# Level 0 of a gated linear attention moved between the last value and gate tiles of the sequence before, with the orders of the other engines

## The reference

```python
q, k, v, gate projections of layernorm(x)
gl = x @ gk_w1 @ gk_w2 + gk_b
g = log_sigmoid(gl) / 16
def step(S, inp):                       # over the 512 tokens, 4 heads
    qt, kt, vt, gt = inp
    S = exp(gt)[:, None] * S + kt[:, None] * vt[None, :]
    return (S, qt @ S)
o = o * rsqrt(mean(o * o) + EPS) * rms_w
o = o.reshape(b, t, DV) * silu(x @ Wg)
x = x + layernorm(o @ Wo)
h = gelu(layernorm(x) @ w1[e] + b1[e]);  y = h @ w2[e] + b2[e]
x = x + layernorm(y)
```

## Time and profile before

| what | us |
|---|---|
| three executions | 1203.73, 1204.50, 1204.88 |
| the profiled execution, its own time | 1204.49 |
| its span, first to last instruction | 1202.7 |
| TensorE busy in the span | 1122.6 (93%) |
| DVE, ACT, POOL busy | 863.7, 810.8, 631.9 |
| odd sequence, even sequence (DVE's L747 to the next) | 72.08, 70.89 (mostly) |
| a bare v or g tile, start to start | 1.38 |
| DVE's wait before q_update(5,0) of run 0 | 0.71 |

### The profile page before, as it was taken

One profiled execution on the slowest core, in us unless ns is written; L12 is line 12 of the kernel. 1 busy time (PEld: TensorE's weight loads), 2 busy tenths in 40 slices (PEclk: granted clock), 3 DMA queues, 4 the chain that ended last, 5 costly groups with the idle time before them and its releaser, 6 DMA issues.

```text
span 1202.7 us, 31412 instructions
## 1 busy us (share of the span) xinstructions
PE 1122.6 (93%) x12368; PEld 916.8 (76%) x12368; DVE 863.7 (72%) x1973; ACT 810.8 (67%) x1749; POOL 631.9 (53%) x906
## 2 busy tenths in 40 slices
PE   3789999999999999999999999999999999999967
PEld 2576878868787787878878687886878878787756
DVE  4649678685876869687685967768587685968653
ACT  5485767777577676866778576777757767586533
POOL 6347355474555645474445735547455564557541
PEclk9789999999999999999999999999999999999988
DMA  3110010100110001200011001010011100110000
GB/s 107 42 36 20 18 54 2 58 20 19 54 46 31 2 18 55 58 20 2 19 55 58 20 19 54 2 58 20 19 54 30 47 3 18 55 58 2 4 16 18
DMA packets 32145, 38.83 MB, mean 32 GB/s; under 512 B 2752, under 2 KB 29440, under 8 KB 32000
## 3 DMA queue, kind: packets, MB, share of 16 engines
q1 hardware_dynamic: 31472, 36.30, 9.2%
q10 hardware_dynamic: 528, 0.52, 0.1%
HBM read 28.43 MB, written 8.39 MB: 31 GB/s over the span
## 4 chain that ended last, share of the span: by engine, by line
PE 67%; ACT 16%; DVE 9%; issue 6%; POOL 1%; DMA 0%; POOLq 0%; ACTq 0%; DVEq 0%
PE ps_big L265 17%; PE ps_big L267 14%; PE ps_big L266 14%; PE ps_out L479 4%; ACT square_out L933 3%; PE ps_level L306 3%; PE ps_level L312 2%; PE ps_out L482 2%; PE ps_state L463 2%; DVE xT_lo L608 2%; ACT L1025 2%; DVE o L665 2%; ACT w_ff_hi L878 1%; ACT out_gate L946 1%; PE ps_transpose L275 1%
## 5 line engine op out<-in xcount | busy, mean ns | idle before, releaser
L1153 POOL TENSOR_TENSOR k_decayed<-k_decayed,block_totals 128x256 f32<-128x256 f32 x192 | 152.7, 797 | 188.3 <-PE ps_level L306 94.9
L638 DVE TENSOR_TENSOR q_blockdiag<-q_blockdiag,block_totals 128x512 f32<-128x512 f32 x192 | 167.1, 870 | 24.8 <-PE ps_level L312 23.1
L1159 POOL TENSOR_TENSOR rstd<-mean_var,minus_half 128x1 f32<-128x1 f32 x192 | 109.6, 573 | 84.4 <-DVE mean_var L676 84.4
L265 PE MATMUL ps_big<-w_ff_hi,h_hi 128*128 128x256 f32 x512 | 150.4, 294 | 0.0
L266 PE MATMUL ps_big<-w_ff_lo,h_hi 128*128 128x256 f32 x512 | 144.6, 282 | 0.0
L267 PE MATMUL ps_big<-w_ff_hi,h_lo 128*128 128x256 f32 x512 | 144.5, 282 | 0.0
L886 ACT ACTIVATE ps_transpose<-ps_big,ff_b_cols 128x512 f32<-128x512 f32 x128 | 84.7, 662 | 57.3 <-PE ps_big L267 55.6
L265 PE MATMUL ps_big<-xT_hi,w_ff_hi 128*128 128x512 f32 x256 | 114.6, 448 | 9.0 <-DVE xT_lo L608 9.0
L306 PEld LDWEIGHTS ps_level<-q_blockdiag,k_decayed 128*32 128x32 f32 x5120 | 56.6, 112 | 73.3 <-DVE q_blockdiag L638 41.1
L265 PE MATMUL ps_big<-w_vg_hi,xT_hi 128*128 128x512 f32 x256 | 108.0, 422 | 0.8
L1183 POOL TENSOR_TENSOR w_ff_lo<-w_raw,w_ff_hi 128x512 fp32r<-128x512 f32 x64 | 96.4, 1508 | 19.0 <-ACT w_ff_hi L878 18.9
(11 more groups left out here) (132 smaller groups left out, 3202.9 us busy)
## 6 DMA issues: line engine op xcount, KB each, us to landing
w_raw<-L_ffn_w SPq DMA_DIRECT2D x16, 1024.0 KB, 6.1
out<-y SPq DMA_DIRECT2D x16, 512.0 KB, 3.2
x_in<-L_attn_x SPq DMA_DIRECT2D x15, 512.0 KB, 3.8
ff_b_rows<-L_ffn_b SPq DMA_DIRECT2D x8, 128.0 KB, 2.1
x_in<-L_attn_x ACTq DMA_DIRECT2D x1, 512.0 KB, 4.3
w_raw<-L_attn_Wv SPq DMA_DIRECT2D x1, 512.0 KB, 5.7
w_raw<-L_attn_Wg SPq DMA_DIRECT2D x1, 512.0 KB, 7.2
y<-L_attn_Wo SPq DMA_DIRECT2D x1, 512.0 KB, 8.1
```

Source lines behind the costliest of these rows:

```text
L265: nc.tensor.matmul(out, ah, bh, start=(first and i == 0), stop=False)
L638: nc.vector.tensor_tensor(q, q, t.to_broadcast([P, 2, T // (2 * h), h]), ALU.mult)\
L1153: nc.gpsimd.tensor_tensor(k, k, t.to_broadcast([P, n, h]), ALU.mult)\
L1159: nc.gpsimd.tensor_tensor(rs[:, k, c:c + 1], mv[:, k, c, 1:2], mhalf[:, 0:1], ALU.pow)\
```

## The change

- TensorE: level 0 of sequence s+1 (`first_level`) is done at the end of run s, its half 0 ahead of vp(3) and its half 1 ahead of gp(3). In the next run x3t comes first, then diag_rows, then the steps from 2 on. f1(m) is at step 2+m (it was 3+m), f2(m) at step 10+m, and xt stands ahead of L(6,1). In run -1 gl comes ahead of kp.
- DVE: the lo parts of x3t stand between the two halves of level 0; the lo parts of h move up by a step; in the tail the two products of q (`q_evac`) are split into `q_times_k` and `q_times_gate`, with og_lo(3) between those of half 0. The second norm of y (ln4(1)) goes behind the norm of x. The w_o rest moves from run -1 to step 9 of run 0.
- ACT: the hi copies of x3t go ahead of the diagonal copy; gelu moves up a step; v(1) goes behind the squares of chunk 3, and ogT_hi(2) ahead of g(1). In the start w_vg_hi goes behind the low-rank copy and the k copies behind Ln; w_o_hi moves to step 5 of run 0, the first w_ff_hi behind xT_hi.
- POOL: the second weights are finished in eight pieces of 128x256 at steps 2 to 9 (four of 128x512 at steps 1 to 4 before). k_update(0,0) stands ahead of the last rstd of the run before, k_update(0,1) behind it. The power of the norm of x goes up a step, and the first expert's rest comes in one piece behind the steps of run 0.
- SP: the first expert's weights wait for two constant matrices instead of three.

```diff
@@ tensor @@
+                def first_level(tl):
+                    pe.wait_ge(sem["ac_qb"], at("ac_qb", n, 2 * (tl + 1)))
+                    pe.wait_ge(sem["dv_q"], at("dv_q", n, 2 * (tl + 1)))
+                    pe.wait_ge(sem["ac_k"], at("ac_k", n, tl + 1))
+                    if B:
+                        pe.wait_ge(sem["dv_t"], at("dv_t", s, 3 + tl))
+                    products(0, tl)
...
-                for step in range(2 * NL):
+                if C:
+                    x3t(0)
+                    x3t(1)
+                if B:
+                    diag_rows()
+                for step in range(2, 2 * NL):
+                    if step == 13 and A:
+                        xt(0)
+                        xt(1)
                     if B:
                         level(step // 2, step % 2)
...
-                        if 3 <= step < 3 + FT:
-                            f1(step - 3)
-                        if 11 <= step < 14:
-                            f2(step - 11)
-                if A:
-                    xt(0)
-                    xt(1)
-                if C:
-                    f2(3)
+                        if 2 <= step < 2 + FT:
+                            f1(step - 2)
+                        else:
+                            f2(step - 10)
...
                 if V:
                     vp(2, n)
                     gp(2, n)
+                if A:
+                    first_level(0)
+                if V:
                     vp(3, n)
+                if A:
+                    first_level(1)
+                if V:
                     gp(3, n)
@@ vector @@
+                        if not C and step == 9:
+                            const_lo(2)
                     if C:
-                        if step == 1:
+                        if step == 0:
                             for kt in range(KT):
...
                 if A:
-                    q_evac(0)
+                    q_times_k(0)
                 if B:
                     og_lo(3)
+                if A:
+                    q_times_gate(0)
+                if B:
                     ln2(2)
@@ scalar @@
                 if V:
                     g_evac(0, n)
-                    v_evac(1, n)
                 if B:
                     o_evac(3)
                     squares(3)
                 if V:
+                    v_evac(1, n)
+                if B:
+                    og_hi(2)
+                if V:
                     g_evac(1, n)
                 if B:
-                    og_hi(2)
                     og_hi(3)
@@ gpsimd @@
-                    w = RAW // 4
+                    w = RAW // (4, 8)[c]
...
-                    if C and j == 1 and 1 <= step < 5:
-                        weight_lo(1, step - 1, e)
-                    if A and step == 12:
+                    if B and step >= 2:
+                        k_update(step // 2, step % 2, s)
+                    if C and j == 1 and 2 <= step < 10:
+                        weight_lo(1, step - 2, e)
+                    if A and step == 11:
...
                 if A:
                     block_totals([6])
+                    pool.wait_ge(sem["po_tot"], at("po_tot", n, NL))
+                    k_update(0, 0, n)
                 if B:
                     rsqrt(2, 3, "dv_ln3", s, "po_p3")
+                if A:
+                    k_update(0, 1, n)
```

More of the change, by code:

```diff
@@ L787, in run @@
                                 const_lo(0)
+                    if C and step == 12:
+                        ln4(1)
                 if A:
@@ L934, in squares, with k_evac @@
                                              accum_out=ssq[:, c * H + hd:c * H + hd + 1]).then_inc(sem["ac_sq"], 1)
+                def k_evac():
+                    for tl in range(KT):
+                        act.wait_ge(sem["pe_k"], at("pe_k", n, tl + 1))
+                        copy(kk[:, tl, :], PB[tl][:, :], "ac_k")
                 def v_evac(c, b):
@@ L963, in og_hi @@
                     copy(ogT_hi[:, :, :], PT[c % 2][:, :].rearrange("p (k t) -> p k t", k=VT), "ac_oghi")
+                if C:
+                    for kt in range(KT):
+                        act.wait_ge(sem["pe_x3t"], at("pe_x3t", p, kt + 1))
+                        copy(xT_hi[:, kt, :], PT[kt][:, :], "ac_x3hi")
                 if B:
@@ L968, in run @@
                 if C:
-                    for kt in range(KT):
-                        act.wait_ge(sem["pe_x3t"], at("pe_x3t", p, kt + 1))
-                        copy(xT_hi[:, kt, :], PT[kt][:, :], "ac_x3hi")
                     act.wait_ge(sem["b_in"], at("b_in", e, 32))
@@ L977, in run @@
                         (v_evac, g_evac)[step % 2](step // 2 - 1, s)
-                    if C and 3 <= step < 3 + FT:
-                        gelu(step - 3)
+                    if B and not C and step == 5:
+                        const_hi(2)
+                    if C and 2 <= step < 2 + FT:
+                        gelu(step - 2)
                     if B and step in (10, 11):
                         expand(step - 10)
-                    if A and j == 0 and step == 11:
-                        weight_hi(0, 0 if not C else e + 1)
+                    if A and C and j == 0 and step == 11:
+                        weight_hi(0, e + 1)
                 if A:
@@ L987, in run @@
                         copy(xT_hi[:, kt, :], PT[kt][:, :], "ac_xhi")
-                    if not B and not C:
-                        act.wait_ge(c_bias, 32)
-                        const_hi(1)
+                    if B and not C:
+                        weight_hi(0, 0)
                 if B:
@@ L997, in run @@
                     copy(gr[:, :], PL[0][:, :], "ac_gr")
+                    if not V:
+                        act.wait_ge(c_bias, 32)
+                        const_hi(1)
                 if B:
@@ L1005, in run @@
                             .then_inc(sem["ac_abs"], 1)
-                    for tl in range(KT):
-                        act.wait_ge(sem["pe_k"], at("pe_k", n, tl + 1))
-                        copy(kk[:, tl, :], PB[tl][:, :], "ac_k")
+                    if V:
+                        k_evac()
                     act.wait_ge(sem["ac_abs"], at("ac_abs", n, KT))
@@ L1198, in run @@
                             late_constants()
-                    if split_w1 and step >= 12:
+                    if split_w1 and C and step >= 12:
                         weight_lo(0, step - 12, next_e)
@@ L1209, in run @@
                 elif split_w1:
-                    weight_lo(0, 2, next_e)
-                    weight_lo(0, 3, next_e)
+                    for part in range(4):
+                        weight_lo(0, part, next_e)
                 if B:
```

77 lines of the change are left out of this document (32 added, 45 removed).

## The result

The changed kernel takes 1217.43 us (median of 4 runs, 1216.84 to 1218.08) against 1204.69 of the kernel before beside it: a ratio of 1.0108, 95% interval 1.009 to 1.0125, slower by 12.7 us. The forecast was 1205.5, the range 1198.5 to 1211.5: wrong, outside the range. The profiled execution took 1216.84, 0.6 under the median, with a span of 1215.1; its span is 12.4 us longer than the 1202.7 before.

What follows compares the result with a forecast made beforehand. The prediction took TensorE as the bound, busy over 69 us of each sequence. Start 1.8 won, odd boundaries 3.4 lost, even boundaries 0.6 won: 1204.5 - 1.8 + 3.4 - 0.6 = 1205.5 us, range 1198.5 to 1211.5.

Steps and rivals of the forecast that it cites:

- Edits at nothing: Small reorderings in the start and later sequences, among them L(6,1) behind xt, each forecast to cost or win nothing.
- Even boundary: Start of runs 2, 4, ... 14: f1(0) 0.63 earlier against 0.55 owed, 0.1 us won, times 7 = 0.6.
- 0.50 to the transposes: Even boundary: time from the start of the last ln3 to TensorE's transposes, taken as 0.50 us.
- The 0.55 owed: Work pushed behind f1(0): L(1,1) 0.38, the diagonal's transpose 0.14 and a rounding, together 0.55 us.
- Odd boundary: Start of runs 1, 3, ... 15: 0.7 + 0.55 + 0.2 - 1.0 = 0.4 us lost, times 8 = 3.4.
- the 0.2 before f2(0): Odd runs: f2(0) waits for the last eighth of the second weights at step 9, taken as 0.2 us.
- Start: The first sequence: 3.4 - 0.8 - 0.8 = 1.8 us won; bounds 4.5 won and 0.7 lost.
- the other 0.8 of the start's sum: Second 0.8 us taken off the start's win of 3.4, besides the 0.8 lost by the norm's chain to kh.
- the hidden boundary: Rival: TensorE, not rstd, is what x3t waits for, and ACT's rounding overlaps; 1196.7 to 1202 us, chance 0.28.
- the lasting lower clock: Rival: the start's lower clock lasts a stretch longer in both places and eats the 3.4; 1207 to 1209, chance 0.12.
- The rival of shared operands: Rival: k_update, q_update and piece overrun 1.97 us per step in odd runs; 1208 us and more, chance 0.22.
- point of failure: Length of a pair of sequences: 143.3 us forecast, 143.0 before; forecast wrong at 142.3 or less, 143.9 or more.

Runs made afterwards that it cites:

- experiment 1: Changed kernel with L(6,1) back ahead of xt on TensorE: 1206.15 us, ratio 1.0014.
- experiment 3: Kernel before with f2(2), xt, L(6,1), f2(3) in that order: 1223.32 us; the same with ln4(1) behind the norm of x: 1214.26 us.
- experiment 4: Changed kernel with ACT's xt hi copies ahead of L(6,1)'s: 1218.52 us; instead with POOL's second first-weights piece ahead of k_update(6,1): 1209.25 us.
- experiment 2: Changed kernel with POOL's pieces of the first weights cut from 512 to 8 columns, part of the computation left out: 1205.76 us, ratio 1.0015.
- experiment 7: Kernel before plus parts: eight second-weight pieces 1196.24 us; these with the start orders 1192.03; tail order alone 1208.23; all three 1198.41.
- the first kernel of experiment 5: Changed kernel with POOL's k_update(0,1) waiting for DVE's ln3(3): 1223.3 us, ratio 1.0159.
- the tail alone: Kernel before with only the new tail order on DVE and ACT (q products split, v(1) and ogT_hi(2) moved): 1208.23 us, ratio 1.0033.
- the second kernel of experiment 5: Changed kernel with L(6,1) back ahead of xt and k_update(0,0) back behind POOL's last rstd: 1205.0 us, ratio 1.0009.

## Why the prediction was wrong, step by step

- **The step that failed** is in "Edits at nothing": "L(6,1) behind xt in later sequences (f2(3) of 2.9 us covers the copies)". It looked at ACT's copies alone. It costs 1.3 us in each even run and 1.6 in the start, 11.3 together (experiment 1; experiment 3 finds 1.2 of the 1.3 in the kernel before). 1.16 of the 1.3 go by k_update(6,1) on POOL, with the pieces and powers queued behind it (experiment 4), and by a DVE norm held for the length of a piece (experiment 2). The remainder was not taken apart. The prediction named neither queue; what L(6,1) releases was not followed past ACT.
- **Even boundary**: 0.1 won was forecast; with L(6,1) back ahead of xt an even run still loses 0.8 (71.66, before 70.89). ln3(3) started 0.54 late as forecast (32.65 behind gl, before 32.11) by the k_update and DVE's share. But "0.50 to the transposes" took the norm as if no POOL product stood beside it: it was 0.97. f1(0) stands 36.28 behind gl instead of 36.46: 0.18 earlier, not 0.63. The sentence "at that time DVE has no q_update to run" asked for the wrong partner; DVE had a norm to run. The 0.55 owed is paid later in the run: from f1(0) to the next gl the kernel of experiment 1 takes 35.42 for 34.42, with a wait of 0.2 at gl in it; 0.25 of this was not taken apart.
- **Odd boundary**: 0.4 lost forecast, 0.2 to 0.3 measured. Each term but one held. f1(0) at 37.21 behind gl instead of 36.64 (0.57, forecast 0.7); the eight pieces give 1.0 (experiment 7, as forecast); the 0.2 before f2(0) didn't come: the last piece (118.74, 0.74 us) ends 0.4 ahead of it (119.91), and a step on POOL takes 0.65 and 0.74 out of 1.98. With the 0.55 owed these make 0.1; what is left of the measured loss was not taken apart. (The prediction's own terms add up to 0.45, or 3.6 in eight runs, where it has 3.4.)

Timeline of the odd boundary after, ACT, TensorE and POOL, for the earlier trace rows:

```profile
100.29 1.92 ACT L897 ACTIVATE w_ff_hi<-w_raw 128x2048 fp32r<-128x2048 f32 x1
102.11 1.07 ACT L897 ACTIVATE xT_hi<-ps_transpose 128x512 fp32r<-128x512 f32 x2
...
104.06 0.50 PE L265 MATMUL ps_big<-xT_hi,w_ff_hi 128*128 128x512 f32 x1 [1.53 <-DVE xT_lo L618]
...
118.74 0.74 POOL L1211 TENSOR_TENSOR w_ff_lo<-w_raw,w_ff_hi 128x256 fp32r<-128x256 f32 x1
```

- **Start**: 1.8 won forecast, 2.9 measured. L(1,0) starts at 30.62, forecast 31.1, before 34.46: 3.8 won. The later part took 1.6 by the moved xt (experiment 1; forecast 0.8 for the norm's chain), and some 0.6 came back in a place not taken apart. No run shows the other 0.8 of the start's sum, held back for the lower clock: the first stretch at 0.50 shrank from 13.6 to 3.4 us, and the second took 10.3 instead of 10.2. Start, for the earlier trace rows:

```profile
30.62 0.66 PE L307 MATMUL ps_level<-q_blockdiag,k_decayed 128*32 128x32 f32 x32
...
55.10 1.97 PE L275 MATMUL ps_transpose<-ident,x_normed 128*128 128x128 f32 x8 [4.61 <-DVE x_normed L704]
```

- **Rivals**: the hidden boundary and the lasting lower clock didn't happen. The rival of shared operands had the right resource and the wrong place and partner: weight pieces and k_updates against DVE's norms at the end of even runs and at the boundary, not against q_update in the odd ones. A pair took 145.34, past the 143.9 that the prediction gave as its point of failure.

## What to carry to other kernels

When a step is moved on one engine, follow what it releases on every engine, and list what is queued behind that instruction there: here an instruction of 1 us on GpSimd, waiting 2 us for a moved product, held three weight pieces and four powers. Filler work of an idle engine belongs ahead of such a wait, not behind it. And where GpSimd and VectorE work at the same time, check every VectorE operation whose operands are in SBUF, the one-input norms too: a norm of 0.4 us takes as long as the GpSimd product that started ahead of it. A bundle of orders is worth taking apart: two of its parts alone won 12 us, and the others lost 25.

## What the runs showed of the hardware

- A DVE tensor_scalar from SBUF to SBUF (128x256, 0.40 alone) took 0.83 and 0.92 beside k_updates of 0.84 and 0.83, and 1.36 beside a weight piece of 1.27. In the changed kernel 91 of the 128 norms of this form started while a product or sum of 128x256 or 128x512 ran on POOL, and each ended 0.14 to 0.22 behind it. The kernel before has 46 of the kind, such as a norm of 0.81 at 209.89 beside a sum of 0.73 at 209.82, so its trace already held the price that the prediction left out. A power of 128x1 on POOL doesn't hold the norm: 0.40 at 206.78, beside one that started at the same time.
- Behind some boundaries with short waits of TensorE the granted clock fell. It was so behind most odd boundaries of the first kernel of experiment 5, six of the tail alone and one of the second kernel of experiment 5: 0.50 (1.2 GHz) for 3.4 us, and the interval grew by 1.4 to 1.5 us. TensorE had waited 2.0 to 2.5 us in two to four pieces there. The sum doesn't decide it: the changed kernel, with 0.94 and 1.53, never showed it, and with the tail alone some boundaries with the same 2.3 didn't. What decides is left open, and so is whether the waits are the cause.
